# The mixer's first norm and its modulation, moved from GpSimd into two VectorE passes

## What is computed

```python
mod = (_silu(L0_c) @ L0_wmod).reshape(16, 6, 1, -1)
sa, ca, ga, sb, cb, gb = (mod[:, i] for i in range(6))
h = _layernorm(x, axis=-1) * (1 + ca) + sa          # first norm and its modulation
x = x + ga * attn_ref(h, ...)
# inside attn_ref:
xn = _layernorm(h, ln1_g, ln1_b)                    # second norm, of h
attn = _windowed_attn(xn, W_qkv, W_O, b_O)          # 16 heads, window 64
ug = xn @ W_ug + b_ug                               # gate, and the drive of a linear recurrence
x = h + g * attn + (1.0 - g) * y_ssm
```

## Time and profile before

| engine | busy us | share of the span | instructions |
|---|---|---|---|
| PE | 2149.6 | 80% | 19260 |
| PEld | 1685.9 | 63% | 19373 |
| DVE | 1466.0 | 54% | 3678 |
| ACT | 936.4 | 35% | 1725 |
| POOL | 1023.9 | 38% | 1184 |

### The profile page before, as it was taken

The page is one execution under the profiler, slowest core; times in us unless marked ns, Lnnn a source line. Parts: engine busy times, 40 slices in busy tenths (PEclk is TensorE's granted clock), DMA queues, the critical chain, the costliest instruction groups (busy, mean ns, idle before and its releaser), DMA issues. The chain is left out here.

```text
span 2692.0 us, 57784 instructions
## 1 busy us (share of the span) xinstructions
PE 2149.6 (80%) x19260; PEld 1685.9 (63%) x19373; DVE 1466.0 (54%) x3678; ACT 936.4 (35%) x1725; POOL 1023.9 (38%) x1184
## 2 busy tenths in 40 slices
PE   1278888888988888889787677677725999999997
PEld 0167766666767766667655445444414888888886
DVE  4155554555454554455466666656633666666664
ACT  0122222222222222222253333333303655656654
POOL 4121121211121121211045565555643666666664
PEclk6599899999999989899898788888857999999998
DMA  3610111111100111110133333333303545554443
GB/s 95 145 34 30 35 35 35 35 35 35 33 9 27 35 35 35 35 35 24 47 113 86 97 97 83 100 82 91 94 27 77 92 91 92 94 92 88 92 92 56
DMA packets 154700, 172.63 MB, mean 64 GB/s; under 512 B 34980, under 2 KB 135975, under 8 KB 154512
## 3 DMA queue, kind: packets, MB, share of 16 engines
q1 hardware_dynamic: 101392, 98.28, 13.1%
q0 software_dynamic: 36352, 56.78, 11.3%
q10 hardware_dynamic: 16896, 16.78, 2.1%
HBM read 109.40 MB, written 53.99 MB: 61 GB/s over the span
## 5 line engine op out<-in xcount | busy, mean ns | idle before, releaser
L1688 POOL DMA_INDIRECT out<-experts_y,experts_entry x144 | 235.6, 1636 | 193.4 <-DVE experts_y L1664 161.4
L569 PE MATMUL mixer_sc<-w_shift,w_select 128*128 128x128 bf16 x1024 | 234.7, 229 | 78.8 <-DVE w_shift L790 76.7
L686 ACT ACTIVATE mixer_prob<-mixer_sc 128x1024 f32<-128x1024 f32 x128 | 131.0, 1023 | 451.7 <-PE mixer_sc L131 451.7
L580 PE MATMUL mixer_pv<-w_V,mixer_prob 128*128 128x33 f32 x2048 | 253.9, 280 | 0.0
L580 PEld LDWEIGHTS mixer_pv<-w_V,mixer_prob 128*128 128x128 f32 x2048 | 245.7, 197 | 1.9
L129 PE MATMUL mixer_sc<-mixer_Qh,w_Kz 128*128 128x128 f16 x1024 | 233.6, 228 | 0.0
L130 PE MATMUL mixer_sc<-mixer_Ql,w_Kz 128*128 128x128 f16 x1024 | 233.3, 228 | 0.0
L131 PE MATMUL mixer_sc<-mixer_Qh,w_Kz 128*128 128x128 f16 x1024 | 232.9, 227 | 0.0
L766 DVE TENSOR_REDUCE w_mx<-mixer_sc 128x4 bf16<-128x512 f32 x256 | 164.8, 684 | 96.4 <-PE mixer_sc L554 94.4
L1301 POOL DMA_INDIRECT scratch_queue<-mlp_entry,mlp_slot x128 | 136.4, 1066 | 201.6 <-DVE mlp_ids L1230 164.7
L1629 DVE TENSOR_SCALAR experts_v<-experts_v 128x512 f32<-128x512 f32 x144 | 75.3, 523 | 218.9 <-ACT experts_v L1603 218.9
(11 more groups left out here) (306 smaller groups left out, 6760.0 us busy)
## 6 DMA issues: line engine op xcount, KB each, us to landing
mixer_x<-in_x SPq DMA_DIRECT2D x16, 512.0 KB, 3.9
scratch_xs<-scratch_mod SPq DMA_DIRECT2D x16, 512.0 KB, 12.7
w_Kz<-mixer_Kt SPq DMA_DIRECT2D x64, 128.0 KB, 2.4
mixer_hres<-mixer_h SPq DMA_DIRECT2D x16, 512.0 KB, 4.8
scratch_x<-mixer_x SPq DMA_DIRECT2D x16, 512.0 KB, 2.9
mlp_xa<-scratch_x SPq DMA_DIRECT2D x16, 512.0 KB, 4.1
mlp_stage<-in_x_w SPq DMA_DIRECT2D x16, 512.0 KB, 5.1
mlp_xb<-scratch_x SPq DMA_DIRECT2D x16, 512.0 KB, 4.9
```

The source lines that it names most:

```text
L569: pe.matmul(out, w["select"][:, var, 4 * c + j, :], w["shift"][:, n % 2, :], start=True, stop=False)
L580: last = pe.matmul(pvO[:, i, :], prob[:, n % 2, i * P:(i + 1) * P], V[:, n, i, :], start=True, stop=True)
L686: act.activation(prob[:, n % 2, :].rearrange("p (c j) -> p c j", c=2), sc[:, 2:4, :], ACT.Exp, scale=SCALE).then_inc(exped.sem, 1)
L1688: pool.indirect_dma_start(out=out, out_offset=bass.IndirectOffsetOnAxis(ap=entry[:, s, t, 0:1].bitcast(I32), axis=0), in_=y[:, s % 2, t, : ...
```

## The change

For x, the call of `normalize` (four instructions L718) goes away. DVE now computes `h` itself in two passes of four `scalar_tensor_tensor` instructions: (x - mean) * (1 + ca), which needs no root, and, after the wait for POOL's root steps, h * rs + sa. Each takes two tensors from SBUF and one scalar per partition. POOL's two wide instructions and its waits for `s_norm0` and `h_kept` are gone. DVE no longer waits for PE's transposes (`xT_mm`) there, since `nrm` isn't written, but for `h_kept`. The counter `s_h` counts 4 per iteration in place of 2.

```diff
-        s_h = m.counter("s_h", 2)
+        s_h = m.counter("s_h", 4)
...
                 if not last:
                     sp.wait_ge(s_norm0.sem, s_norm0.at(b, 4))
-                    sp.wait_ge(s_h.sem, s_h.at(b, 2))
+                    sp.wait_ge(s_h.sem, s_h.at(b, 4))
                     load(b + 1)
-                sp.wait_ge(s_h.sem, s_h.at(b, 2))
+                sp.wait_ge(s_h.sem, s_h.at(b, 4))
...
+        def scale_and_shift(dve, b):
+            dve.wait_ge(h_kept.sem, h_kept.at(b, 0))
+            for t in range(TT):
+                dve.scalar_tensor_tensor(out=h[:, t, :], in0=x[:, t, :], scalar=mv[:, t, 0:1], in1=shsc[:, 1, :],
+                                         op0=ALU.subtract, op1=ALU.mult).then_inc(s_norm0.sem, 1)
+            dve.wait_ge(s_rstd.sem, s_rstd.at(b, NEWTON))
+            for t in range(TT):
+                dve.wait_ge(s_norm0.sem, s_norm0.at(b, t + 1))
+                dve.scalar_tensor_tensor(out=h[:, t, :], in0=h[:, t, :], scalar=rs[:, t:t + 1], in1=shsc[:, 0, :],
+                                         op0=ALU.mult, op1=ALU.add).then_inc(s_h.sem, 1)
...
             if part == 2:
-                dve.wait_ge(xT_mm.sem, xT_mm.at(b, 0))
-                normalize(dve, b, x, 0, s_norm0)
+                scale_and_shift(dve, b)
             if part == 5:
-                dve.wait_ge(s_h.sem, s_h.at(b, 2))
+                dve.wait_ge(s_h.sem, s_h.at(b, 4))
                 moments(dve, b, h, 1)
...
             def modulate(b):
                 inverse_deviation(b, 0)
-
-                pool.wait_ge(s_norm0.sem, s_norm0.at(b, 4))
-                pool.wait_ge(h_kept.sem, h_kept.at(b, 0))
-                pool.tensor_tensor(h[:], nrm[:], shsc[:, 1:2, :].to_broadcast([P, TT, D]), ALU.mult
-                                   ).then_inc(s_h.sem, 1)
-                pool.wait_ge(s_h.sem, s_h.at(b, 1))
-                pool.tensor_tensor(h[:], h[:], shsc[:, 0:1, :].to_broadcast([P, TT, D]), ALU.add
-                                   ).then_inc(s_h.sem, 1)
                 inverse_deviation(b, 1)
```

## The result

The kernel after takes 2728.14 us (median of four runs, 2725.04 to 2733.33), against 2697.54 for the kernel before beside it (four runs, 2691.14 to 2701.16). The ratio is 1.0118, with a 95% interval of 1.0091 to 1.0145: slower by 31 us, where 2705.8 was forecast and 2720 was the upper end of the range. In the ratios of four experiments (`pad2`, `pe_busy6`, `after_again`, `after_late`), which share their runs of the kernel before, one such run of 8910.55 us, in the slow state, isn't counted.

The account below looks back on a forecast made before the run. Bound by step 2's chain of root steps, DVE's work on x, copy L790, PE. 0.30 + 0.05 + 0.30 = 0.65 us, 15 bodies, 9.8 us, prologue and clock 0: 2705.8 us by the median; range 2696 to 2720.

Parts of the forecast that it names:

- Where the chain ends, and who holds it: Mixer step 2: root steps, DVE's work on x, copy L790, then PE; 0.65 us longer per body, 15 bodies, 9.8 us.
- Second pass: Step 2, in place of L718: four instructions take 1.68 us, so the copy comes 0.30 us later; bounds 0 and 0.4.
- Contention: Step 2: DVE's first pass and POOL's root steps take turns, making the root 0.30 us late; bounds 0 and 1.4.
- Rival (a): Step 2: POOL gets no turn until the first pass ends; 1.75 us per body, 26 us, 2722 us; chance 0.09.
- Second wait: Step 2: DVE's added wait for `s_norm0` after the root wait costs 0.05 us; bounds 0 and 0.15.
- PE's idle: Step 2: PE's stall for the copy L790 grows from 1.87 to 2.5 us.
- The wait for `h_kept`: Ahead of the first pass: DVE's new wait costs 0, as the copy to `hres` lands with 2.3 us to spare.
- POOL's wide work: Two POOL instructions of 2.34 us per body vanish; nobody waits for them in the 15 bodies, so 0 us gained.
- The prologue: Before body 0's attention: first transposes come 4.6 us earlier, but key copies wait for SP; gain 0, bounds -4.6 and 0.
- key copies still at 126.1: Body 0: SP issuing the key copies at an unchanged time was named a sign of being right.
- The clock: Behind step 2: PE's mix of granted clocks, 3 bodies at 1.00, 8 at 0.76–0.79, 4 at 0.50–0.60, stays; 0 us.
- Rival (b): Behind step 2: longer stall turns half of eight bodies at 0.77 to 0.50; 22 us, 2718 us; chance 0.18.

Follow-up runs that it names:

- pad2: Kernel before with two more instructions like L718, results thrown away, behind step 2's root wait: 2730.58 us, 1.0113.
- pe_busy6: Kernel before with PE doing six of its value matmuls (L580) twice in step 3, right behind the stall: 2722.27 us, 1.0101.
- after_again: The kernel after, unchanged, measured again in ten runs against the kernel before: 2726.35 us, 1.0104.
- after_late: Kernel after with the second pass and its root wait moved from step 2 to step 3: 2650.18 us, 0.9822 of the kernel before.
- after_gates: Kernel after with SP's 16 gate copies moved behind body 0's copy to `hres`: 2714.21 us, 1.0078 of the kernel before.
- pad1: Kernel before with one more instruction like L718, result thrown away, in step 2 (0.32 us more stall): 2728.1 us, 1.0103.
- fill_after: Kernel after with eleven useless 512-column matmuls (2.35 us) in PE's idle of step 2: 2682.2 us, 0.9975 of the kernel before.
- fill_busy6: Kernel before with six extra value matmuls in step 3 and eight useless matmuls in PE's idle of step 2: 2723.86 us, 1.0094.
- the pads: Kernel before with one, two or four more instructions like L718 in step 2, results thrown away: 1.0103, 1.0113 and 1.0154.

## Why the prediction was wrong

**Where the chain ends, and who holds it: right.** 0.64 us a body were measured, 0.65 forecast. The terms came out at 0.29, 0.27 and 0.10 for 0.30, 0.30 and 0.05 forecast; that their errors cancel to a hundredth is luck.

- Second pass: 1.67 us against 1.68 worked out from the earlier trace rows, 0.29 more than L718.
- Contention: from the first root step's start to the last one's end it is 4.66 us (1241.29 to 1245.95) in place of 4.39 (1207.16 to 1211.55), so 0.27, against 0.30. The rows show the turns that were drawn from the earlier trace rows: one step of 0.42 (0.22 late, 0.24 forecast), the others delayed by some hundredths or not at all. Rival (a) is dead.
- Second wait: from the last root step's end to DVE's start it is 0.13 us (1245.95 to 1246.08) in place of 0.03, so 0.10, against 0.05 and within its bounds.
- PE's idle: 2.52, against 2.5. DVE's root wait: 1.71, against some 1.5.
- The wait for `h_kept`: no idle of DVE ahead of the first pass, as said.
- POOL's wide work: gone, and nobody gained, as said.

**The prologue: right in its reason, and one sign missed.** SP's gate copies hide the gain; the rows of `after_gates` show it when they are gone. The rows of SP and PE in body 0:

```profile
87.52 41.41 SPq L497 DMA_DIRECT2D scratch_xs<-scratch_mod  x16
128.98 5.98 SPq L482 DMA_DIRECT2D w_Kz<-mixer_Kt  x4
...
144.00 0.61 PE L552 MATMUL mixer_sc<-w_maskq,w_twoI 128*128 128x512 bf16 x1 [18.10 <-DMA w_Kz<-mixer_Kt]
```

DVE was through with the keys at 122.03 (120.75 + 1.28), 3.4 us earlier than before, and SP issued them at 128.98 and not at 126.08: it began its gate copies 1.2 us later and took 1.7 us longer for them. PE waits 18.10 us. These 2.9 us were in neither bound, and key copies still at 126.1 had been named as a sign of being right. They are this execution's own: in `after_again` SP issues the key copies at 126.80 and PE starts at 141.77, half a microsecond behind the kernel before.

**The clock: wrong, and this is the step that failed.** "In the forecast the mix stays." It didn't: behind step 2 the bodies at 0.50 went from three to six, and those between 0.50 and 1.00 sank from 0.64–0.79 to 0.58–0.71. The term for the clock stood at 0 in the sum. What the runs showed in its place: over bodies 1 to 14 a remainder of 21.7 us in the profiled pair, of which 41 us more at 0.50 explain 18.6, and by the medians 21 (30.6 less 9.6 for the chain). Rival (b) had the mechanism and some 60% of the price (12.4), as it counted only bodies that change kind, and it got 0.18. What misled me was the argument against it: three bodies with the same stall had different clocks, from which I drew that 0.6 us of stall couldn't matter. `pad1` shows that 0.3 us does. The same rows could have been read the other way: kinds that sit side by side under equal stalls may be near an edge, and a change of stall in all 15 bodies at once can tip many of them. And 68 us of low clock around step 2 were there to be read in the kernel before, nearly all begun within PE's idle of that step; that called for a price, not for zero.

**What stays open.** That idle in step 2 costs clock is shown from both sides, by adding it (`pad2`) and by filling it (`fill_after`), and the low clock of `pe_busy6` and `fill_busy6` lies behind another idle, that of step 1. That three filling matmuls beat eleven is explained by what the filling costs at 0.50. What isn't shown is which idle is followed by a low: of equal idles of 1.94 us in step 1, one in 14 in the kernel before and all 14 in `pe_busy6`. So neither the steps of the pads (23, 20 and 22 us for 5, 10 and 20 us of stall) nor the number of lows in a new kernel can be worked out from these runs. Why the lows around the 3.45 us idle went from 85 to 68 us with the change is open too.

## What to carry to other kernels

Where PE's granted clock is under 1.00 behind a recurring stall, a longer stall on the critical path has two prices, its own length and the clock of the work behind it; here the second was twice the first (some 20 us beside 10). Read the time at 0.50 in the whole body, not only behind the place that was changed: a longer body moves the other idles too. Put the pure delay into the old kernel, as `pad2` did, and what the delay costs comes apart from what the new instructions cost, in one run. If an idle is filled, fill less than its length, as the filling takes nearly twice as long where the clock is already low (2.54 and 4.35 us for eleven matmuls). And look at what the piece on the path waits for before asking who should compute it: to move the piece one step behind its root wait was worth 44 us in the kernel before (0.9838) and 76 in the kernel after (1.0104 to 0.9822), while the change of engine, with that done, was worth nothing that can be measured.

## What the runs showed of the hardware

Useless work can make a kernel faster: three matmuls of 0.64 us a body in an idle of 2.5 us gave 56 us back in the kernel after (ratios 1.0104 and 0.9896). A pad of 0.3 us a body cost as much clock as one of 1.3, within the intervals (219 and 207 us at 0.50). The granted clock goes to 0.50 within a PE idle of 1.87 us, before its end, in 11 of 14 bodies of the kernel before. The DMA issues of SP aren't of a fixed length: the same 16 gate copies held its queue for 39.68 us in one execution and for 41.41 in another.
